# Edge loop in bodies of six chunks, with a third fetched row set in every third chunk

## What is computed

```
h_fwd = h @ W_forward.T                 # h: layer norm of x, 6250 x 256; result 6250 x 64
h_rev = h @ W_reverse.T
messages = h_fwd[src] * direction[:, 0:1] + h_rev[src] * direction[:, 1:2]
scores = leaky_relu(messages @ attn_forward[0].T, 0.2)      # 4 heads
exp_scores = exp(scores - scores.max(axis=0))
norm = exp_scores / (segment_sum(exp_scores, dst)[dst] + 1e-10)
out[:, hd] = segment_sum(messages * norm[:, hd:hd + 1], dst)  # for each of 4 heads
```

## Time and profile before

| | |
|---|---|
| profiled execution | 2466.73 us |
| its span, first to last instruction | 2465.0 us |
| median of 3 runs | 2465.9 us |
| PE, DVE, POOL, ACT busy | 2005.7, 1856.6, 1633.1, 357.6 us |
| POOL, gathers of the edge stage, line 262 | 1375 |
| PE, matmuls of the fetches, line 978 | 5264 |
| mean granted TensorE clock | 0.900 |

### The profile page before, as it was taken

The page is one execution under the profiler, slowest core; times in us unless marked ns, Lnnn a source line. Parts: engine busy times, 40 slices in busy tenths (PEclk is TensorE's granted clock), DMA queues, the critical chain, the costliest instruction groups (busy, mean ns, idle before and its releaser), DMA issues.

```text
span 2465.0 us, 44434 instructions
## 1 busy us (share of the span) xinstructions
PE 2005.7 (81%) x11977; PEld 1744.4 (71%) x11978; DVE 1856.6 (75%) x4481; ACT 357.6 (15%) x1034; POOL 1633.1 (66%) x1757
## 2 busy tenths in 40 slices
PE   7588888888888888888788888888547599999970
PEld 6477777777777777777677777777546588888860
DVE  5787887878787878787878787878658856666657
ACT  4100000000000000000000000000025433434335
POOL 6777777777777777777777777777737743333327
PEclk9699999999999999999999999999755599999995
DMA  6222222222222222222222222222325765555557
GB/s 209 60 66 62 66 62 66 64 63 64 64 64 63 64 64 63 64 64 63 64 63 64 64 66 62 66 62 66 111 90 164 252 201 200 187 190 198 202 170 269
DMA packets 176304, 256.65 MB, mean 104 GB/s; under 512 B 47078, under 2 KB 120999, under 8 KB 176004
## 3 DMA queue, kind: packets, MB, share of 16 engines
q0 software_dynamic: 53696, 121.60, 18.8%
q1 hardware_dynamic: 122564, 134.56, 17.6%
HBM read 218.11 MB, written 38.79 MB: 104 GB/s over the span
## 4 chain that ended last, share of the span: by engine, by line
POOL 38%; issue 25%; DVE 15%; PE 9%; DMA 6%; DVEq 5%; SPq 2%; ACT 1%; POOLq 0%; ACTq 0%
POOL rows L262 37%; DVEq L1716 3%; PE p_win L882 3%; DMA rows<-node_table,index 3%; DVE p_part L1006 2%; PE p_y L1884 1%; DVE p_y L1939 1%; PE p_h L1874 1%; DVE hot_ex L1038 1%; DVE second L1919 1%; DVE hid_t L1911 1%; PE p_hot L978 1%; DVE back L1924 1%; DMA out<-shared 1%; DVE rows L1003 1%
## 5 line engine op out<-in xcount | busy, mean ns | idle before, releaser
L262 POOL DMA_INDIRECT rows<-node_table,index x1375 | 1301.4, 946 | 445.5 <-issue 417.8
L978 PE MATMUL p_hot<-parts,onehot 128*128 128x476 f32 x5264 | 1194.5, 387 | 12.3 <-DVE rows L1071 12.3
L978 PEld LDWEIGHTS p_hot<-parts,onehot 128*128 128x128 f32 x5264 | 1003.5, 192 | 174.9 <-issue 19.0
L882 PE MATMUL p_win<-hot_ex,msg 128*65 128x64 f32 x3136 | 261.1, 256 | 272.9 <-DVE hot_ex L1038 268.9
L882 PEld LDWEIGHTS p_win<-hot_ex,msg 128*65 128x65 f32 x3136 | 246.5, 170 | 310.9 <-issue 310.9
L1056 DVE TENSOR_TENSOR onehot<-key,p_dve 128x896 fp32r<-128x896 f32 x188 | 203.4, 1082 | 108.5 <-PE p_hot L978 105.4
L1725 POOL DMA_INDIRECT expert_rows<-ys,back x104 | 103.1, 992 | 270.7 <-DVE ys L1944 196.2
L932 ACT ACTIVATE p_dve<-score,neg_shift 128x64 f32<-128x64 f32 x98 | 31.1, 318 | 1681.2 <-DVE score L1023 1681.2
L1066 DVE SCALAR_TENSOR_TENSOR p_hot<-place_no,place_of_source,p_hot 128x476 f32<-128x476 f32 x376 | 250.0, 710 | 0.0
L997 DVE TENSOR_TENSOR shared<-shared,p_win 65x64 f32 x784 | 170.0, 217 | 106.0 <-PE p_win L882 15.9
L1003 DVE TENSOR_TENSOR rows<-rows,p_dve 128x1088 f32<-128x1088 f32 x98 | 126.1, 1287 | 137.2 <-DMA rows<-node_table,index 137.1
(11 more groups left out here) (269 smaller groups left out, 1422.4 us busy)
## 6 DMA issues: line engine op xcount, KB each, us to landing
shared<-in_w SPq DMA_DIRECT2D x120, 512.0 KB, 3.8
rows<-node_table,index POOLq DMA_INDIRECT x1375, 2.8
xs<-dispatched SPq DMA_DIRECT2D x104, 129.5 KB, 3.5
key<-hot_keys SPq DMA_DIRECT2D x94, 128.0 KB, 3.1
shared<-expert_rows SPq DMA_DIRECT2D x12, 896.0 KB, 8.2
token_rows<-in_x SPq DMA_DIRECT2D x7, 896.0 KB, 12.9
shared<-in_x SPq DMA_DIRECT2D x7, 768.0 KB, 9.0
out<-shared SPq DMA_DIRECT2D x6, 896.0 KB, 7.8
```

The costliest lines, as they stand in the source:

```text
L262: pool.indirect_dma_start(out=rows[:, s, k, :], out_offset=None, in_=table, in_offset=bass.IndirectOffsetOnAxis(ap=index[:, s, 0, k:k + 1] ...
L882: last = pe.matmul(psum[0:MSG, u * HEADS * W:(u + 1) * HEADS * W], msg[:, k, :], weighted[:, k, :, :].rearrange("p h w -> p (h w)"), start ...
L978: last = pe.matmul(p_hot[:, j, d, 0:PLACES * COLS], onehot[:, j, gr, :], parts[:, gr:NT:GP, m, d * COLS:(d + 1) * COLS], start=(gr == 0 an ...
```

## The change

The chunks fetched by PE take 2, 2, 3, 2, 2, 3 ... sets by `CYCLE`, the three where the chunk's number leaves 2 when divided by 3 (chunks 2, 5 ... 95). POOL gathers 13 sets of these, 14 of the others. The loop's body has six chunks (`BODY`, so that the cycle and the two buffers both come out even) and 15 turns; chunks 0 and 1 and the last six are written out. Counts that were products of the turn are now read from tables (`of`).

PE fetches all sets of chunk c+1 ahead of the sums of chunk c. A fetch is cut in a forward and a reverse half (`fetch_half`); the second half of a third fetch is left for the next step, ahead of its sums. DVE's order depends on the chunks that come: where c+2 has three, its first set is built at the start and kept at the end of c's step. `key` holds three keys, and SP loads as many as the chunk has. The list of fetched sources grows from 192 to 222 (220 used).

```
+CYCLE = (2, 2, 3)
+BODY = len(CYCLE)
+while BODY % RING or sum(CYCLE) * BODY // len(CYCLE) % 2:
+    BODY += len(CYCLE)
+TURNS = (NCH - 3 * RING) // BODY
+LOOPED = RING + TURNS * BODY
+FILLS = [CYCLE[c % len(CYCLE)] for c in range(NCH - RING)] + [0] * RING
+FETCHED = [sum(FILLS[RING:c]) for c in range(NCH + 1)]
+SETS = [KG] * RING + [K - n for n in FILLS[RING:NCH - 1]] + [K_LAST]
...
+                steps(range(begun, RING), None)
+                with eng.Fori(0, TURNS) as turn:
+                    steps(range(RING, RING + BODY), turn)
+                steps(range(LOOPED, NCH), None)
...
             @block.gpsimd
-                    sets = K_LAST if final(c) else K if whole(it) else KG
+                    sets = SETS[p[0]]
...
             @block.sync
-                    if not whole(it):
-                        sp.wait_ge(hot_built, FILL * (c - 1))
-                        sp.dma_start(key[:, s, :, :], keys[ds(c * FILL, FILL), :].partition_broadcast(P))\
+                    if fetched_of(p):
+                        sp.wait_ge(hot_built, of(BUILT_BY, p, -1))
+                        n = fetched_of(p)
+                        sp.dma_start(key[:, s, 0:n, :], keys[ds(of(FETCHED, p), n), :].partition_broadcast(P))\
                           .then_inc(key_ready[s], 16)
...
             @block.tensor
-                    if coming(s, it, 1, 1):
-                        fetch(*coming(s, it, 1, 1))
+                    if fetched_of(p) == 3:
+                        fetch_half(p, 0, 2, 1)
+                    for j in range(fetched_of(p, 1)):
+                        fetch_half(p, 1, j, 0)
+                        if j < 2:
+                            fetch_half(p, 1, j, 1)
                     pe.wait_ge(msg_ready, c + 1)
                     pe.wait_ge(val_ready, c + 1)
                     after(pe, added, UPC * c)
                     sum_units(pe, p_win[:, :], hot_ex[:, :, :, :], UPC).then_inc(summed, 1)
                     extra_sums(c, loaded[s])
-                    if coming(s, it, 2, 0):
-                        fetch(*coming(s, it, 2, 0))
...
-                def fetch(f, s, it, j):
-                    after(pe, hot_kept, 2 * (f - FILL + 1))
-                    pe.wait_ge(hot_built, HOT + f + 1)
+                def fetch_half(p, ahead, j, d):
+                    f = of(FETCHED, p, ahead) + j
+                    v = place_of(p, ahead, j)
+                    if d == 0:
+                        after(pe, hot_kept, 2 * (f - 1))
+                        pe.wait_ge(hot_built, f + PREBUILT + 1)
                     for gr in range(GP):
                         for m in range(2):
-                            for d in range(2):
-                                last = pe.matmul(p_hot[:, j, d, 0:PLACES * COLS], onehot[:, j, gr, :],
+                            last = pe.matmul(p_hot[:, v, d, 0:PLACES * COLS], onehot[:, v, gr, :],
...
-                    last.then_inc(hot_rows, 1)
+                    if d == 1:
+                        last.then_inc(hot_rows, 1)
...
             @block.vector
-                    if coming(s, it, 2, 0):
-                        build_hot(*coming(s, it, 2, 0))
-                    all_rows(dve, c, s, it)
+                    near, far = fetched_of(p, 1), fetched_of(p, 2)
+                    if far == 3:
+                        build_hot(p, 2, 0)
+                    if near == 3:
+                        build_hot(p, 1, 2)
+                    all_rows(dve, p, s)
...
-                    if coming(s, it, 1, 0):
-                        keep(*coming(s, it, 1, 0))
-                    if coming(s, it, 1, 1):
-                        keep(*coming(s, it, 1, 1))
-                    finish(c)
-                    if coming(s, it, 2, 1):
-                        build_hot(*coming(s, it, 2, 1))
+                    if near == 3:
+                        keep(p, s, 1, 1)
+                        if far:
+                            build_hot(p, 2, 0)
+                        finish(c)
+                        keep(p, s, 1, 2)
+                        if far:
+                            build_hot(p, 2, 1)
+                    elif far == 3:
+                        for j in range(near):
+                            keep(p, s, 1, j)
+                        finish(c)
+                        build_hot(p, 2, 1)
+                        keep(p, s, 2, 0)
+                    else:
+                        if near:
+                            keep(p, s, 1, 0)
+                        if far:
+                            build_hot(p, 2, 0)
+                        if near:
+                            keep(p, s, 1, 1)
+                        finish(c)
+                        if far:
+                            build_hot(p, 2, 1)
```

More of the change, by code:

```diff
@@ L70 @@
 EXTRA = 8192
-assert HOT == FILL * RING and FILL == 2 and EARLY < RING and NF % 3 == 0 and UPC * HEADS * W <= 512
+SETS = [KG] * RING + [K - n for n in FILLS[RING:NCH - 1]] + [K_LAST]
+GATHERED = [sum(SETS[c % RING:c + 1:RING]) for c in range(NCH)]
+TURN_OF_SLOT = [c // RING for c in range(NCH)]
+NUMBER = list(range(NCH))
+assert HOT == FILL * RING and FILL == 2 and EARLY < RING and UPC * HEADS * W <= 512
+assert BODY % RING == 0 and BODY % len(CYCLE) == 0 and LOOPED + 2 * RING <= NCH and all(2 <= n <= 3 for n in CYCLE)
+assert all(a + b < 6 for a, b in zip(FILLS, FILLS[1:])) and NF // 3 <= P
 assert K_LAST > EARLY_SETS
@@ L418, in _ @@
                 late = hot_late[0:NF // 3, 0, :, :]
-                rest, step = (spare[:, 6 * P + m * NF:6 * P + (m + 1) * NF] for m in range(2))
+                rest, step = (spare[:, x_at - (m + 1) * NF:x_at - m * NF] for m in range(2))
                 pool.tensor_copy(source, source.bitcast(I32)).then_inc(s_init, 1)
@@ L856, in fill_of, with steps @@
[L856 to L866, removed]
+                def steps(chosen, turn):
+                    for b in chosen:
+                        if b % RING == 0 or b == begun:
+                            loaded = begin((b - b % RING, turn))
+                        step((b, turn), b % RING, loaded)
@@ new lines, in chunks, with of @@
+                steps(range(begun, RING), None)
+                with eng.Fori(0, TURNS) as turn:
+                    steps(range(RING, RING + BODY), turn)
+                steps(range(LOOPED, NCH), None)
+            def of(table, p, ahead=0):
+                b, turn = p
+                b += ahead
+                if turn is None:
+                    return table[b]
+                grows = table[b + BODY] - table[b]
+                assert all(table[b + (i + 1) * BODY] - table[b + i * BODY] == grows for i in range(TURNS - 1))
+                return turn * grows + table[b]
@@ new lines, in final, with fetched_of, place_of @@
+            def final(p):
+                return p == (NCH - 1, None)
+            def fetched_of(p, ahead=0):
+                b, turn = p
+                if not RING <= b + ahead < NCH - RING:
+                    return 0
+                return FILLS[b + ahead]
+            def place_of(p, ahead, j):
+                b, turn = p
+                f = FETCHED[b + ahead] + j
+                assert turn is None or (FETCHED[RING + BODY] - FETCHED[RING]) % 2 == 0
+                return f % 2
@@ L1058, in build_hot @@
+                def build_hot(p, ahead, j):
+                    f = of(FETCHED, p, ahead) + j
+                    t, v = (p[0] + ahead) % RING, place_of(p, ahead, j)
+                    dve.wait_ge(key_ready[t], 16 * of(TURN_OF_SLOT, p, ahead))
+                    after(dve, hot_rows, f - 1)
+                    dve.tensor_tensor(onehot[:, v, :, :],
+                                      key[:, t, j, :].unsqueeze(1).broadcast_to([P, GP, P]),
                                       group_p.unsqueeze(2).broadcast_to([P, GP, P]), ALU.is_equal)\
@@ L1059, in build_hot, with keep @@
                        .then_inc(hot_built, 1)
-                def keep(f, s, it, j):
+                def keep(p, s, ahead, j):
+                    f = of(FETCHED, p, ahead) + j
+                    t, v = (s + ahead) % RING, place_of(p, ahead, j)
+                    first = K - fetched_of(p, ahead)
                     dve.wait_ge(hot_rows, f + 1)
-                    found = p_hot[:, j, :, 0:PLACES * COLS].rearrange("p d (v c) -> p d v c", v=PLACES)
+                    found = p_hot[:, v, :, 0:PLACES * COLS].rearrange("p d (v c) -> p d v c", v=PLACES)
@@ L2175 @@
     by_chunk = np.ascontiguousarray(attr.transpose(2, 0, 1, 3))
-    src_hot = src.reshape(NIT, RING, P, K)[1:, :, :, KG:].transpose(0, 1, 3, 2).reshape(NF, P)
+    fetched = [src[c, :, k] for c in range(RING, NCH) for k in range(K - FILLS[c], K)]
+    src_hot = np.stack(fetched + fetched[0:NF - NHOT])
     arrays = {
```

107 lines of the change are left out of this document (47 added, 60 removed).

## The result

The changed kernel took 2502.5 us, median of four runs (2499.5 to 2504.9), beside 2466.7 us for the kernel before on the same chip: ratio 1.0147, interval 1.0135 to 1.0159. The forecast was 2430, with a range of 2423 to 2463: wrong in sign. The profiled execution has a span of 2503.1 us.

A forecast was written before the change was run, and what follows sets the result against it. POOL's gathers were taken to bound the edge loop, before and after. Terms 40.0 + 1.8 - 0.9 - 2.4 - 2.5 = 36.0 us less took 2466.7 to 2430.7, set at 2430 us; range 2423 to 2463.

The forecast's parts named there:

- Rival 2: PE or DVE refetch the longer loop body's code at each jump back: 2440, 2466 or 2491 us; chance 0.14.
- the dearest of the three prices: Code refetch at a loop jump on PE or DVE, priced at 1.7, 3.4 or 5.1 us a turn.
- The rival's formula: Loss over the loop's 15 turns, 15 x (s - 1), s being the refetch price and about 1 us covered.
- The rule cited with it: Skill's rule: a taken branch outside the pages held forces a fetch and stalls; 128 KiB for TensorE, unconfirmed by runs.
- POOL's 40.0 us: Gain in the edge loop from 32 fewer POOL gathers at 1.251 us each.
- The long gap, 1.8 us,: One of POOL's 2.1 us gaps, every 112 gathers, pushed past the loop's end: 1.8 us gained.
- the walk: Path round PE, DVE and POOL over three chunks: 18.2, 17.8 and 15.7, together 51.7 us against POOL's 51.95.
- Rival 1: Loop of PE and DVE becomes the bound, 52.2 to 53.0 us in three chunks: 2438 to 2463 us; chance 0.24.
- meshing: Imperfect meshing of two loops 0.25 us apart: 0.08 us in three chunks, 2.5 us lost (bounds 0 and 9).
- The start, 0.9 and 2.4 us.: Losses before the loop: 0.9 us for loading a third key, 2.4 us for the early keep delaying POOL's gather.
- Rival 3, the clock,: PE falls to 1.2 GHz once in three chunks, adding 2.8 us each time: 2507 us; chance 0.05.

The follow-up runs named there:

- e10: Changed kernel with 160 never-executed matmuls and their weight loads ahead of PE's edge loop, so its body lies further on: 2421.5 us, ratio 0.9832.
- e11: e8 (the rotated kernel) with 64 never-executed matmuls and their 64 weight loads ahead of PE's loop: 2447.0 us, ratio 0.9933.
- e8: Changed kernel with PE's loop boundary rotated by half a step, sums first in the body and fetches last: 2417.3 us, ratio 0.9813.
- e4: Changed program with two fetched sets in every chunk and a body of two chunks, keeping PE's new order: 2472.1 us, ratio 1.0021.
- e12: e5 with two fetches in every chunk but still 13 gathers in every third, leaving one row set out there: 2406.1 us, ratio 0.9768.
- e5: Changed kernel without the never-entered code for extra windows on PE and DVE (short code): 2413.5 us, ratio 0.9798.
- e9: Changed kernel with PE's program alone written out for all 98 chunks, other engines keeping their loop: 2409.7 us, ratio 0.9786.
- e1: Changed kernel with the edge loop written out chunk by chunk, so nothing jumps back: 2417.7 us, ratio 0.9802.
- e2: Changed kernel with twelve chunks in the loop body and 7 turns instead of 15: 2446.1 us, ratio 0.9918.
- e6: Kernel before, with its own order and two sets in every chunk, but six chunks in the body and 15 turns: 2466.1 us, ratio 0.9997.
- e7: Kernel before with its edge loop written out on all engines, order of work unchanged: 2462.7 us, ratio 0.9996.

## Why the prediction was wrong, step by step

- **The failing step.** Rival 2, "slower, by code", was the right mechanism, set aside with "against it: PE's queue still holds the sums when the jump comes". It holds less than a microsecond of them: the first branch starts at 224.7, the sums ahead of it end at 223.43 + 2.10 = 225.53, and the branch takes 4.1 us.

```profile
223.43 2.10 PE L902 MATMUL p_win<-hot_ex,msg 128*65 128x64 f32 x32 [0.23 <-DVE hot_ex L1072]
229.85 16.99 PE L1007 MATMUL p_hot<-parts,onehot 128*128 128x476 f32 x70 [4.31 <-issue]
```

  In the turn shown above PE stood 3.95 - 0.23 = 3.7 us longer than at other steps and then lost 17.95 - 15.6 = 2.35 us to the low clock, 6.1 us together. Over all 14 jumps the pause is 4.14 us and the fetch behind it 17.39 us on average, 5.7 us together; that is more than the dearest of the three prices (5.1). e10 and the changed kernel differ by 1.0147 - 0.9832, 78 us, 5.6 a jump: nearly all of it reaches the end, where the rival took about 1 us of each turn as covered. The rival's formula would give 15 x (5.7 - 1) = 71 us; its price was too low and its cover too large, and the chance of 0.14 followed from the step above.
- **What the rows would have allowed.** Whether the code is held was left as a chance. 0.26 MB in 16 packets gives the unit of 16 KB, and the body of six is three times a body of two. That hints that the body is several packets long and that the limit matters; whether it is held, and at which place, no row of before could tell.
- **The rule cited with it.** The Trainium skill (Runtime: NRT & Kernel Launch, Instruction fetch mechanics) gives TensorE 128 KiB, refilled in blocks of 16 KiB, the next one fetched ahead. The runs fit that for PE as far as they go: the changed kernel and e11 load 9 packets of 16 KB in every turn, 144 KB, more than that size, and e8 and e10, with the same body at another place, hold it all. Between the loop's start and the first jump PE asks for 7 packets in the changed kernel and in e11 and for 6 in e8, but for 7 in e10 too, the first of them 0.5 us behind the loop's start; so a count of blocks as the limit is argued, the effect of the place is shown. The section also has a taken branch stall when its target lies outside a window of two pages; the jumps of e8 and e10 go back over 6 or 7 packets in 0.2 us, so that does not hold for PE here.
- **POOL's 40.0 us** was right in count (1343 gathers); a gather took 952 ns instead of 946, in e4 too, 8 us over all, cause open.
- **The long gap, 1.8 us,** was mis-sized. All 12 are gone, 12 x 1.8 = 22 us. e12 against e4 gives POOL's part by itself: 1.0021 - 0.9768, 62 us, by 40.0 + 22.
- **DVE, PE and the walk** were right as far as the runs tell. PE's sums in e5 follow each other by 18.33, 17.35 and 15.7 to 15.8 us, 51.4 to 51.5 in three chunks; the walk said 18.2, 17.8 and 15.7, 51.7. POOL's 41 gathers, 1.257 us apart in e5, take 51.5, so this shows that the walk is no longer than POOL's pace, not its own length. Rival 1 did not come, and meshing cost nothing that the waits show: POOL waits 15.9 us for score and sums in e5's 1400 us, 20.4 before.
- **The start, 0.9 and 2.4 us.** Chunk 2's products come at 130.27 instead of 125.1, 5.2 us against 3.3; 3.1 of it lie before chunk 0's products (94.70 for 91.6), where kernels with the same code there differ as much (91.4 in e9, 94.5 in e8); what is left, 2.1 us, is less than forecast. The three starts in the changed kernel, answering to the earlier trace rows:

```profile
94.70 1.28 DVE L1037 TENSOR_TENSOR rows<-rows,p_dve 128x1088 f32<-128x1088 f32 x1
...
111.70 1.34 DVE L1122 SCALAR_TENSOR_TENSOR p_hot<-place_no,place_of_source,p_hot 128x476 f32<-128x476 f32 x2 [3.52 <-PE p_hot L1007]
...
130.27 1.28 DVE L1037 TENSOR_TENSOR rows<-rows,p_dve 128x1088 f32<-128x1088 f32 x1
```

- **Rival 3, the clock,** came as a consequence: once a turn, behind the 3.95 us pause. With the pause gone (e10) no stretch of the loop from 150 to 1650 us is below 1.00.
- **The net.** With the code held, the change as it stands gives 0.9832, near the forecast's 0.9854, but that is luck, errors against each other: some 20 us more gained from the gaps, some of it lost again at the start, by the longer gathers and by DVE's jump.

The versions that beat both kernels with the whole computation are e9 (0.9786), e1 (0.9802), e8 (0.9813) and e10 (0.9832), and by less e2 (0.9918) and e11 (0.9933).

## What to carry to other kernels

A longer loop body is not free because its steps fit: count the code of each engine's body in the blocks that its instruction queue loads, and after the change look for that queue's packets inside the loop and at the branch's duration, on every engine. Where they appear, moving the loop's boundary or writing the loop out on the one engine that pays can give everything back without a change to the schedule. A rival that is dismissed by "the queue will cover it" should be set against the length of what stands in the queue.

## What the runs showed that was not expected

- 160 matmuls that are never executed, with their weight loads, made the changed kernel 78 us faster (e10 against it), and 64 made the rotated one 30 us slower (0.9933 - 0.9813).
- The reload is all or nothing for PE within a turn: 9 packets or none with six chunks in the body. In e6, in the same program, it came at 4 of 15 turns; why at those stays open.
- PE pays dearly for it and DVE hardly: DVE reloads 6 packets of 8 KB each turn in e8 and e10 and stands 1.8 to 1.9 us on average, of which at most 0.4 us a turn reach the end.
- The 2 us gap of POOL at every 112th gather, steady through all kernels with 14 gathers in each chunk (before, e4, e6, e7), vanishes with 13 in every third.
